# Graph network kernel: head layer and the last layer's scatter in one program

## What is computed

```
x = _layernorm(x + _L0_gnn_ref(...))   # per relation attention
x = _layernorm(x + _L1_gnn_ref(...))   # messages: two dense layers per edge, summed by dst
x = _layernorm(x + _L2_gnn_ref(...))   # eight heads: softmax over the edges of a dst, sum of v
x = _layernorm(x + _L3_gnn_ref(x, edge_weight, src, dst))   # (x + 3 * spmm) / 4
```

```
gathered = vals[:, None] * x[cols]                    # vals = edge_weight, cols = dst
segment_sum(gathered, rows, num_segments=n)           # rows = src
```

## Time and profile before

| | us |
|---|---|
| median of 3 runs | 2985.21 |
| the runs | 2978.31, 2985.21, 2987.78 |
| profiled execution, its own time | 2977.81 |
| its span | 2976.0 |
| busy of the span: PE, DVE, ACT, POOL | 2145.4, 1681.6, 934.6, 1713.8 |
| granted clock of TensorE, mean | 0.656 |

### The profile page before, as it was taken

The page is one execution under the profiler, slowest core; times in us unless marked ns, Lnnn a source line. Parts: engine busy times, 40 slices in busy tenths (PEclk is TensorE's granted clock), DMA queues, the critical chain, the costliest instruction groups (busy, mean ns, idle before and its releaser), DMA issues. The chain is left out here.

```text
span 2976.0 us, 39029 instructions
## 1 busy us (share of the span) xinstructions
PE 2145.4 (72%) x10407; PEld 1742.6 (59%) x10407; DVE 1681.6 (57%) x4134; ACT 934.6 (31%) x2602; POOL 1713.8 (58%) x1705
## 2 busy tenths in 40 slices
PE   5448888888685899799954677776846766565377
PEld 2337777777664778687734665665743443343277
DVE  4257777777412233843424666777776855555366
ACT  2356666665111334244323222222200000000044
POOL 3477777770002777877717777766303777777700
PEclk9655555555555999899975555555555656666589
DMA  5755555440102333233315444443201322222165
GB/s 204 255 149 147 148 148 148 141 143 24 36 18 62 93 88 99 64 100 97 83 49 157 138 135 137 136 124 110 84 7 54 85 82 82 80 83 83 60 219 175
DMA packets 245376, 321.82 MB, mean 108 GB/s; under 512 B 106223, under 2 KB 161284, under 8 KB 243814
## 3 DMA queue, kind: packets, MB, share of 16 engines
q0 software_dynamic: 66560, 163.90, 19.3%
q1 hardware_dynamic: 178566, 155.09, 17.5%
HBM read 257.86 MB, written 62.54 MB: 108 GB/s over the span
## 5 line engine op out<-in xcount | busy, mean ns | idle before, releaser
L2464 POOL DMA_INDIRECT rows_by_src<-e_weighted,e_row x416 | 420.3, 1010 | 278.0 <-DVE e_weighted L2368 162.2
L1259 POOL DMA_INDIRECT e_gathered<-msg_src_table,src_idx x416 | 420.6, 1011 | 275.9 <-POOLq L364 149.5
L1759 POOL DMA_INDIRECT e_kv<-kv_table,src_idx x416 | 415.2, 998 | 215.1 <-issue 120.0
L630 POOL DMA_INDIRECT e_gathered<-rel_src_table,rel_idx x416 | 431.2, 1037 | 178.7 <-issue 124.3
L1840 PE MATMUL e_ps_a<-e_onehot,e_weighted 128*128 128x66 f32 x832 | 199.6, 425 | 143.2 <-DVE e_onehot L2001 143.2
L1840 PEld LDWEIGHTS e_ps_a<-e_onehot,e_weighted 128*128 128x128 f32 x832 | 184.3, 328 | 167.6 <-DVE e_weighted L1997 165.8
L673 PE MATMUL e_ps_r<-e_window,e_spread 64*128 64x128 f32 x832 | 215.2, 437 | 75.6 <-DMA e_window<-rel_dst_table 35.7
L687 PE MATMUL e_ps_a<-e_typed,e_rel 128*128 128x72 f32 x832 | 206.0, 429 | 79.8 <-DVE e_typed L815 79.8
L1821 PE MATMUL e_ps_q<-e_window,e_spread 64*128 64x128 f32 x832 | 211.2, 432 | 49.8 <-ACT e_spread L1932 30.5
L687 PEld LDWEIGHTS e_ps_a<-e_typed,e_rel 128*128 128x128 f32 x832 | 185.1, 327 | 105.0 <-DVE e_typed L815 88.8
L673 PEld LDWEIGHTS e_ps_r<-e_window,e_spread 64*128 64x128 f32 x832 | 185.1, 325 | 100.0 <-issue 59.0
(11 more groups left out here) (445 smaller groups left out, 4582.4 us busy)
## 6 DMA issues: line engine op xcount, KB each, us to landing
n_rows<-rows_by_src SPq DMA_DIRECT2D x26, 1032.0 KB
e_offsets<-group_offsets SPq DMA_DIRECT2D x208, 128.0 KB
e_keys<-tile_keys SPq DMA_DIRECT2D x104, 128.0 KB
e_window<-rel_dst_table SPq DMA_DIRECT2D x416, 32.0 KB
e_mixed<-in_edge_attr_dram SPq DMA_DIRECT2D x103, 128.0 KB
rel_src_table<-t_up SPq DMA_DIRECT2D x5, 2560.0 KB
e_gathered<-rel_src_table,rel_idx POOLq DMA_INDIRECT x416
e_gathered<-msg_src_table,src_idx POOLq DMA_INDIRECT x416
```

The costliest lines, as they stand in the source:

```text
L630: pool.indirect_dma_start(gathered[:, q % GS, j, :], None, rel_table, bass.IndirectOffsetOnAxis(ap=rel_idx[:, q * J + j:q * J + j + 1], ax ...
L1259: pool.indirect_dma_start(gathered[:, q % GS, j, :], None, msg_table, bass.IndirectOffsetOnAxis(ap=src_idx[:, q * J + j:q * J + j + 1], ax ...
L1759: pool.indirect_dma_start(kv[:, q % RING, j, :], None, kv_table, bass.IndirectOffsetOnAxis(ap=src_idx[:, q * J + j:q * J + j + 1], axis=0) ...
L2464: pool.indirect_dma_start(in_order, bass.IndirectOffsetOnAxis(ap=row[:, q // 2 % RS, q % 2 * J + j:q % 2 * J + j + 1], axis=0), weighted[: ...
```

## The change

The blocks `head_layer` and `propagate` become one, `head_and_rows`. Its parts:

- POOL sends its 416 scatters right after its 416 gathers, from the same ring `kv`, whose slots now take the weighed rows (columns 0 to 128). Scatter q waits for its row (`taken`), tag and place.
- The groups of the last layer ("rows") are expanded from turn 102 on (`first_row`), group q in turn 102 + q, beside the remaining sums and the updates of blocks 3 and 4. They use the same windows, spreads (made on ScalarE) and PSUM banks as the head's groups.
- Marking and counting of ranks: pairs 0 to 3 in turns 100 to 103, pair 4 in turn 110, then every second turn; placing one turn later. One PSUM bank in place of two, shared with the softmax.
- The last chunk has 13 groups; one sum per turn up to turn 121; the seven parts of a node block stand in every second turn: block 3 in turns 109 to 121, block 4 in turns 123 to 135.
- `onehot` of the head's sums is made on ScalarE (four Abs, one Relu) in place of VectorE.
- `lay_out` tests with `SAFE` too that rows of group q touch only blocks stored by then.
- `messages` counts one bound per turn, in turns 12 to 60, with one instruction that accumulates, in place of seven comparisons and seven reductions; it also makes the bucket of each edge.
- The buckets' bases are made in small pieces from turn 116 on. Several tiles share memory.

The core of the diff:

```diff
@@ lay_out
+SAFE = [E // N * GN * (g + 1) // GE - 3 for g in range(NG - 1)] + [Q - 1]
...
+                        dve.tensor_scalar(late[:, NG + g:NG + g + 1], rows[0:1, 0, SAFE[g]:SAFE[g] + 1], float(GN * (g + 1) - REACH), float(GE), ALU.is_gt, ALU.mult).then_inc(reached, 1)
@@ messages
-                def compare(n):
-                    hold(dve, below_made, n)
-                    dve.tensor_tensor(lower[:, :, :], src_t[:, :].unsqueeze(1).to_broadcast([P, PART, T]),
-                                      bounds[:, n * PART:(n + 1) * PART].unsqueeze(2).to_broadcast([P, PART, T]), ALU.is_lt).then_inc(lowered, 1)
-
                 def count(n):
-                    dve.wait_ge(lowered, n + 1)
-                    dve.tensor_reduce(below[:, n * PART:(n + 1) * PART], lower[:, :, :], AX.X, ALU.add).then_inc(below_made, 1)
+                    hold(dve, below_made, n - 1)
+                    dve.tensor_scalar(lower[:, n % 2, :], src_t[:, :], float(BUCKET * n), 0.0, ALU.is_lt, ALU.add,
+                                      accum_out=below[:, n:n + 1]).then_inc(below_made, 1)
...
+                    if t in range(FIRST_BOUND, FIRST_BOUND + NB):
+                        count(t - FIRST_BOUND)
@@ head_layer, now head_and_rows
-            SIZES = [CH] * (NCH - 1) + [8, 5]
+            SIZES = [CH] * NCH
...
-                t = max(SOFT_AT[chunk_of[p][0]] + 4, total_at[-1] if total_at else 0)
-                while total_at.count(t) >= (1 if t < AT[NCH - 1] + 5 else 2):
-                    t += 1
-                total_at.append(t)
...
+                total_at.append(max(SOFT_AT[chunk_of[p][0]] + 4, total_at[-1] + 1 if total_at else 0))
+            totals = dict(zip(total_at, range(Q)))
+
+            def first_row(early):
+                return Q - 2 if early else total_at[Q - 1] + 2 + 7 * NG
...
-                    at = max(total_at[READY[g] if early else Q - 1] + 2, at + 1)
+                    at = max(total_at[READY[g] if early else Q - 1] + 2, SOFT_AT[PARTS - 1] + 4 if early and g == NG - 2 else 0, at + 1)
+                    stride = 2 if early else 1
                     for part in range(7):
-                        steps[at + part] = (g, part)
-                    at += 6
+                        steps[at + stride * part] = (g, part)
+                    at += stride * 6
...
+            def expansions(t, early):
+
+                row_group = t - first_row(early)
+                return ([(False, t)] if 0 <= t < Q else []) + ([(True, row_group)] if 0 <= row_group < Q else [])
...
+            def count_of(t, early):
+
+                s0 = first_row(early)
+                if early and t < s0 + 2 * SAID:
+                    return t - (Q - 4) if 0 <= t - (Q - 4) < SAID else None
+                return (t - s0) // 2 if t >= s0 and (t - s0) % 2 == 0 and (t - s0) // 2 < Q // 2 else None
...
+            def send_rows(pool, early):
+                number = numbers(early)
+                for q in range(Q):
+                    slot = (Q + q) % RING
+                    pool.wait_ge(taken, number[True, q] + 1)
+                    pool.wait_ge(tagged, q + 1)
+                    pool.wait_ge(placed, q // 2 + 1)
+                    pool.nop(nofuse=True)
+                    for j in range(J):
+                        pool.indirect_dma_start(in_order, bass.IndirectOffsetOnAxis(ap=row[:, q // 2 % RS, q % 2 * J + j:q % 2 * J + j + 1], axis=0),
+                                                kv[:, slot, j, 0:D + 1], None).then_inc(sent[slot], 16)
...
+                    if rows:
+                        if q == 0:
+                            sp.wait_ge(pads_stored, 16 * 4)
+                        for g in range(NG):
+                            if q == (SAFE[g - 1] + 1 if early and g else 0):
+                                sp.wait_ge(own_stored[g], 16)
...
+                        sp.dma_start(window[0:gw, at % WS, :], (x_last if rows else q_window)[bass.ds(base + w * gw, gw), :]).then_inc(win_in[at % WS], 16)
...
+                def count(u):
+                    s = u % 2
+                    flat = lambda a: a.rearrange("p b t -> p (b t)")
+                    pe.wait_ge(attn_ready, PARTS - 1 if early and u < SAID else PARTS)
...
+                    pe.wait_ge(carried, u + 1)
...
+                    hold(pe, chosen, u)
...
+                    pe.matmul(flat(ps_k), minus_after[:, :], flat(inside[:, s, :, :]), start=True, stop=False)
...
+                def mark(p):
+                    hold(act, summed, nw * (p - 1))
+                    for j in range(J):
+                        far = act.activation(onehot[:, p % 2, j, :], marks[:, :], ACT.Abs, bias=part_t[:, p * J + j:p * J + j + 1], scale=-1.0)
+                    far.then_inc(apart_made, 1)
+                    act.wait_ge(apart_made, p + 1)
+                    act.activation(onehot[:, p % 2, :, :], onehot[:, p % 2, :, :], ACT.Relu, bias=1.0, scale=-1.0).then_inc(marked, 1)
...
+                def weigh_row(q):
+                    n = number[True, q]
+                    dve.wait_ge(expanded, nw * (n + 1))
+                    slot_free(dve, Q + q)
+                    dve.tensor_tensor(kv[:, (Q + q) % RING, :, 0:D], ps_q[n % 2][:, :, :],
+                                      w_t[:, q * J:(q + 1) * J].unsqueeze(2).to_broadcast([P, J, D]), ALU.mult).then_inc(taken, 1)
...
-                    dve.tensor_tensor(onehot[:, p % 2, :, :], marks[:, :].unsqueeze(1).to_broadcast([P, J, REACH + 2]),
-                                      part_t[:, p * J:(p + 1) * J].unsqueeze(2).to_broadcast([P, J, REACH + 2]), ALU.is_equal).then_inc(marked, 1)
...
+                    for rows, q in expansions(t - 1 if nw == 1 else t, early):
+                        (weigh_row if rows else score)(q)
+                    turn = count_of(t - 1, early)
+                    if turn is not None:
+                        place(turn)
...
+                    turn = count_of(t, early)
+                    if turn is not None:
+                        mark(turn)
...
-    def propagate(below, first_bucket, bucket_base):
```

452 lines of the change are left out of this document (196 added, 256 removed).

## The result

| | before | after |
|---|---|---|
| median, us | 2983.82 of 4 runs (2978.31 to 2987.78) | 2889.43 of 4 runs (2886.95 to 2892.59) |
| profiled execution's own time | 2977.81 | 2892.59 |
| its span | 2976.0 | 2890.8 |
| granted clock of TensorE, mean | 0.656 | 0.671 |

The ratio after to before is 0.9685, with a 95% interval of 0.9666 to 0.9705: 94 us less between the medians. Between the two profiled executions the difference is 85.2, because the profiled execution of before (2977.81) lies under all its four runs and that of after is the highest of its four. What follows is counted between these two.

A forecast was written before the change was run, and what follows sets the result against it. POOL was taken to work at its own pace around a 151.6 us hole before the first scatter. 0.5 - 11.5 - 65 + 1 = -75, with less scatter stretching -78: from 2985.21 to 2907 us, range 2862 to 2948.

The forecast's parts named there:

- the first rival: Scatters: POOL never starves after its first row, PE's clock being at its upper level; 2871 to 2832, say 2862; chance 0.17.
- Head turns: Head layer: one-hot on ScalarE cuts turns from 4.72 to 4.38 us, 19 us; four single-sum turns win 8 more.
- the slower rival: Head sums: marking on ScalarE becomes the bound, turns of 5.8 us or more, kernel at 3027; chance 0.04.
- First ranks and the hole: Turns 100 to 103: 6.2, 10.3, 10.3 us; first row weighed about 2137; POOL idle some 30 us, not 151.6.
- the parts ahead: Before the head: layout's four extra VectorE instructions, 0.5 us more, and the messages' edge counting, -11.5 us.
- The overlap: Rows beside sums and node updates, until POOL sets the pace; last scatter at 2756, not 2821.5: 65 us, head gains included.
- Three stretches of rows: Overlap turns 103 to 109, 109 to 122 and 122 to 136: 43, 116 and 92 us.
- the rival in which it is fed all through: The first rival: POOL never starves after its first row; say 2862 us; chance 0.17.
- The rival in which the overlap eats most: Overlap: node-update parts wait behind count and sum, some 14 x 3 us, head turns unchanged (+19); 2955 or so; chance 0.17.
- Messages: Messages layer: gathers freed of long comparisons save 16.5 us, 49 counts cost 5 back: -11.5, between -16.5 and +3.5.
- The boundary: End of the joined program: POOL waits on 24 slots instead of 4 and more semaphores are cleared, +1 us.
- the 3 for shorter scatters: Scatters: a few us less stretching because the spreading leaves VectorE, taking the sum from -75 to -78.

The follow-up runs named there:

- the experiment with the places: Changed kernel with VectorE picking places behind the weighing from the fifth pair on: 2879.37 us, against 2896.36 for the changed kernel run again.
- the short comparison: Changed kernel with each count split into a comparison without accumulation and a reduction: 2895.10 us, against 2896.36 for the changed kernel run again.
- the kernel with the old comparisons: Changed kernel with the seven comparisons and reductions back in messages: 3502.78 us on the third chip, 3499.01 on the second; ratios 0.9797 and 0.9749 to before.

## Why the prediction was right, point by point

Forecast 2907 from 2985.21, so -78; measured 2889.43 from 2983.82, a change of -94, inside the range (2862 to 2948) and on the side of the first rival. The mechanism was right part by part; the largest term was too dear by 19 us, and no error the other way was of that size.

*Head turns.* Right: 4.72 to 4.32 us, against 4.38 forecast. To the product of group 95 the head took 555.2 us before and 535.4 now, from its first gather: 19.8, forecast 19. At 0.4 us a turn the forecast's 56 turns would give 22; the rest is lost in turns that something else lengthens. ScalarE's Abs was cheaper than its bound (337 ns, not 389), and PE now waits for the weighing and for nothing else:

```profile
L1926 PE MATMUL e_ps_a<-e_onehot,e_weighted 128*128 128x66 f32 x832 | 200.9, 421 | 129.3 <-DVE e_weighted L2173 129.3
...
L2032 ACT ACTIVATE e_onehot<-marks,part_t 128x66 f32<-128x66 f32 x416 | 110.7, 337 | 107.2 <-PE e_ps_a L1926 107.1
```

So the slower rival, the marking as the bound, had no place: ScalarE waited for PE, not PE for it.

*First ranks and the hole.* Right: turns of 8.3 and 9.4 us where 10.3 was forecast, the first row weighed at 2126.35, the first scatter at 2127.87 (forecast near 2126: 2137 less the 11 of the parts ahead), the hole 30.6 us (some 30).

*The overlap*, the largest term, was too long by 19 us. Three stretches of rows: 36 us (forecast 43), 106 (116), 90 (92). The first two are the terms mis-sized. I had taken turns with softmax or two sums as they were; they have one sum and no one-hot now, which I take for the reason that they are shorter. And for a pair in the sum phase I had 13.8 us, with PE's sum and count one behind the other at the head's clock. Windows of after (as the earlier trace rows: busy and count of PE, PEld, DVE, ACT, POOL, then PEclk):

```profile
1900.00:2000.00 100.00, 77.08 (x303) 64.93 (x302) 73.13 (x171) 49.68 (x122) 75.78 (x79) 0.53 0.47 136
2180.00:2300.00 120.00, 75.99 (x265) 52.31 (x264) 75.86 (x203) 37.04 (x93) 66.07 (x62) 0.64 0.19 58
2490.00:2710.00 220.00, 122.44 (x432) 77.98 (x431) 90.55 (x170) 51.78 (x112) 168.80 (x169) 0.71 0.27 78
```

In the overlap POOL starts 62 scatters in 120 us, 7.7 us per group of four (forecast 7 to 8) where its own pace is 5.2, so it is fed two thirds of the time: the rival in which it is fed all through did not come true. But of its reason a part did: the granted clock there is 0.64 of full speed, not 0.50 to 0.53, between the levels of 1.2 and 2.4 GHz. The rival in which the overlap eats most did not come either; the experiment with the places shows that its mechanism is real, VectorE in order behind a wait for the count, at 17 us rather than the 42 (14 parts of 3 us) I gave it. (With the 19 of the head turns that rival comes to 2968, not to the 2955 I wrote, and so lay outside my range; nothing measured hangs on it.) I had costed that wait inside the pair, and had not named it as what could be taken out. Behind the overlap 169 scatters start in 220 us, 5.21 per group, against 5.19 forecast.

*Messages.* Forecast -11.5, measured -16.4: the 5 us set against the counts did not appear. The 49 counts run from 1030.2 to 1275.3; the gathers between 1200 and 1275 have a mean of 966 ns, against 1312 in the earlier trace rows. By the rule of the Trainium skill ("SBUF — State Buffer", section "SBUF: two separate sides") that I weighed there, a VectorE instruction in a two-port mode blocks GpSimd for its length, and one with two SBUF inputs does so against a GpSimd instruction that reads SBUF. The comparisons of the earlier trace rows have two such inputs, and their gathers bear out the second half. For the first half the short comparison is the test: it and the gathers did wait for each other, but only in part of the gather's length and by 0.23 us at most, so that a mean of 978 ns against 974 was all that came of it.

*Around it.* The boundary costs more than the 1 us forecast: from the last scatter to the load of the sorted rows it is now 16.4 us (2732.2 to 2748.58), before 12.4 (2820.49 to 2832.85), so 4 of it from the end of the joined program, and 2.9 us more lie ahead of the head's first gather, which I did not foresee. Which of the longer set-up's instructions these are was not tried.

*The sum.* From the head's first gather to the last scatter the gain is 81.9 us where I had 68: 19 more from the overlap, 4 more up to the first row, less 7, since from row 33 to the last scatter it is 375 us and not 368, and less the 3 for shorter scatters, which did not come (1018 ns for 1010). The messages give 5 more. Against them stand 2 for the boundary, 3 for the set-up and 7 before the messages, most of which is probably not the change's. That makes -85 between the profiles for -78; between the medians 9 more, because the profiled execution of before lies 6 us under its median and that of after 3 above its own. So the last 9 of the 94 are the choice of executions, and part of the closeness of -85 to -78 is luck: 28 us of gain and 22 of cost that I had not foreseen stand against each other.

## What to carry to other kernels

When two stages on an in-order queue are joined, the gain is not the hole but the hole less what the second stage's start costs while it runs beside the first: here 147 us at the first scatter, 88 at the last, because the overlap runs at VectorE's pace. Look at the order of the instructions that wait in that overlap: placing a wait behind the work that others wait for was worth 17 us, and it took no work away. And price an operation by the turn it stands in: 0.4 us on VectorE comes to some 20 us of the head layer where VectorE's turn is the pace, and to 1 and 6 up to the first scatter on the two chips with other waits in the turns.

## What the runs showed that I had not expected

The form of a small VectorE instruction changes its price more than what it does to POOL. The count of 416 fp32 elements with accumulation takes 576 ns, and 82 ns more to read the accumulator; the same comparison without it mostly 365 to 368.

What holds POOL is not the long comparison alone (2.87 to 3.73 us for a gather of 0.94). The scatters meet it all through the rows, in before and after alike. One stretch of after:

```profile
2504.82 0.97 POOL L1815 DMA_INDIRECT rows_by_src<-e_kv,e_row  x1 [0.30 <-issue]
2504.83 0.69 DVE L2102 TENSOR_TENSOR e_kv<-e_ps_q,w_t 128x512 f32<-128x512 f32 x1
2506.03 0.97 DVE L2113 TENSOR_TENSOR_SCAN e_tally<-e_renew,e_inside 128x392 f32<-128x392 f32 x1
2506.09 1.69 POOL L1815 DMA_INDIRECT rows_by_src<-e_kv,e_row  x1 [0.30 <-issue]
```

Of the 28 scatters that had the scan of the marking (L2113, two inputs in SBUF) beside them 0.13 us after their start, 24 took over 1.1 us; of the 45 that had the weighing of a row there (L2102, one input in PSUM), none. Together the 416 scatters take 22 us more than 0.965 each, which is about the length of an undisturbed one. By this estimate VectorE's two-input instructions stand for 0.2 us in POOL's 5.2 per group. No run takes them away.

And the second and third chip ran all these kernels some 600 us slower, at nearly the same clock (0.633 to 0.646 against 0.664 to 0.667 in the profiles of the edited kernels) and with POOL's gathers no longer than elsewhere (960 ns). Their profiles show the difference in waits named "remote", in front of SP's loads of windows among others (354.6 us at one line). PE, VectorE and ScalarE together spend 1132 to 1451 us in such waits there and none on the first chip. What they are could not be told from the profiles. The gain of the change seems to be as large there: on the third chip the kernel with the old comparisons, 3502.78, less 14.5 is some 3488, and before is 3579.4.
